# Two conditional residual layers on one core: layer 0 as four 64x64 array tiles, two pairs per block and two pairs ahead

## The reference

```python
# layer 0, per batch b: subject s = itok_B_0_7[b] of 8
x = x + einsum('bct,bcd->bdt', x, weights[s]) + bias[s][:, :, None]   # weights[s]: 64 x 64
# layer 1, per batch b: adapter a = itok_B_0_6[b] of 8
H = einsum('btd,od->bto', x, W)                                      # W: 512 x 512
xa = einsum('btd,brd->btr', x, A[a])                                 # rank 16
delta = einsum('btr,bor->bto', xa, Bm[a]) * scalings[a]
x = x + H + delta
```

## Time and profile before

| | us |
|---|---|
| three executions | 275.54, 275.44, 274.51 |
| median | 275.44 |
| span of the profiled execution, first to last instruction | 271.8 |
| PE busy in that span | 256.0 |
| DVE busy | 148.6 |
| ACT busy | 113.3 |
| POOL busy | 87.9 |

### The profile page before, as it was taken

The page is one execution under the profiler, slowest core; times in us unless marked ns, Lnnn a source line. Parts: engine busy times, 40 slices in busy tenths (PEclk is TensorE's granted clock), DMA queues, the critical chain, the costliest instruction groups (busy, mean ns, idle before and its releaser), DMA issues.

```text
span 271.8 us, 6814 instructions
## 1 busy us (share of the span) xinstructions
PE 256.0 (94%) x1393; PEld 220.1 (81%) x1394; DVE 148.6 (55%) x244; ACT 113.3 (42%) x189; POOL 87.9 (32%) x285
## 2 busy tenths in 40 slices
PE   0598999999999999999999999999999999999993
PEld 0476888888888888888888888888888888888882
DVE  5668677555655556555665566555655553344300
ACT  2254554433544354433444353443434433323511
POOL 7355223433333332333432342333332333330000
PEclk9999999999999999999999999999999999999998
DMA  6662554454554545444554455543655455455221
GB/s 122 160 164 59 158 145 144 129 148 123 168 137 134 153 135 154 136 134 133 170 141 129 141 144 154 146 128 114 171 147 143 131 152 156 138 144 148 63 55 39
DMA packets 25821, 36.62 MB, mean 135 GB/s; under 512 B 6736, under 2 KB 8784, under 8 KB 25808
## 3 DMA queue, kind: packets, MB, share of 16 engines
q1 hardware_dynamic: 20400, 28.06, 37.1%
q10 hardware_dynamic: 5408, 8.40, 11.9%
HBM read 19.67 MB, written 16.78 MB: 134 GB/s over the span
## 4 chain that ended last, share of the span: by engine, by line
PE 91%; DVE 3%; DMA 3%; ACT 1%; issue 1%; SPq 0%; ACTq 0%; DVEq 0%
PE ps L696 66%; PE ps L682 21%; PE ps L671 3%; DMA a_f<-in_L_cond_A_dram 2%; DMA ids_i<-in_itok_B_dram 1%; PE ps L653 1%; DVE x_lo L494 1%; DVE m_lo L481 1%; PE ps L643 0%; ACT x_hi L559 0%; DVE prec_n L382 0%; DVE a_parts L460 0%; DVE m_f L475 0%; ACT m_hi L553 0%; ACT a_parts L542 0%
## 5 line engine op out<-in xcount | busy, mean ns | idle before, releaser
L696 PE MATMUL ps<-m_hi,x_hi 128*128 x264 | 108.6, 411 | 0.8 <-DVE x_lo L494 0.4
L696 PE MATMUL ps<-m_lo,x_hi 128*128 x264 | 103.1, 390 | 0.0
L696 PE MATMUL ps<-m_hi,x_lo 128*128 x264 | 103.1, 390 | 0.0
L353 POOL COPY p_pair<-p_all 64x64 f32 x128 | 52.0, 406 | 149.8 <-issue 73.3
L682 PEld LDWEIGHTS ps<-p_pair,x_ring 128*128 128x128 f32 x512 | 67.5, 193 | 5.4 <-DMA x_ring<-in_x_dram 0.4
L494 DVE TENSOR_TENSOR x_lo<-x,x_hi 128x512 fp32r<-128x512 f32 x64 | 44.5, 695 | 47.1 <-ACT x_hi L559 47.1
L682 PE MATMUL ps<-p_pair,x_ring 128*128 128x128 f32 x512 | 68.1, 276 | 0.0
L568 ACT ACTIVATE o_ring<-ps 128x512 f32<-128x512 f32 x60 | 35.8, 596 | 74.2 <-PE ps L696 74.0
L487 DVE TENSOR_TENSOR x<-ps,bias_pair 128x512 f32<-128x512 f32 x64 | 44.2, 691 | 35.9 <-PE ps L682 35.2
L559 ACT ACTIVATE x_hi<-x 128x512 fp32r<-128x512 f32 x64 | 40.5, 632 | 43.3 <-DVE x L487 43.3
L696 PEld LDWEIGHTS ps<-m_hi,x_lo 128*128 128x128 f32 x264 | 49.6, 188 | 10.6
(11 more groups left out here) (82 smaller groups left out, 54.5 us busy)
## 6 DMA issues: line engine op xcount, KB each, us to landing
x_ring<-in_x_dram SPq DMA_DIRECT2D x128, 128.0 KB, 2.6
out_dram<-o_ring SPq DMA_DIRECT2D x64, 128.0 KB, 2.6
out_dram<-o_ring ACTq DMA_DIRECT2D x64, 128.0 KB, 2.3
o_ring<-in_L_cond_W_dram SPq DMA_DIRECT2D x4, 256.0 KB, 4.4
a_f<-in_L_cond_A_dram SPq DMA_DIRECT2D x8, 128.0 KB
b_nat<-in_L_cond_Bm_dram SPq DMA_DIRECT2D x1, 256.0 KB, 4.0
p_all<-in_L_cond_weights_dram SPq DMA_DIRECT2D x2, 128.0 KB, 4.2
bias_all<-in_fside_8xS_dram SPq DMA_DIRECT2D x1, 256.0 KB, 4.7
```

Of the source, the lines that this page charges most:

```text
L353: nc.gpsimd.tensor_copy(p_pair[rows, slot, rows], p_all[rows, ds(s[half], 1), :] .rearrange("p s d -> p (s d)")).then_inc(pair_ready, 1)
L696: mm = nc.tensor.matmul(ps[:, bank, :], part[:, u % 2, c, :], m[:, ds(k * (TC * T) + c * T, T)], start=(c == 0 and part is x1_hi and m is ...
```

## The change

`layer0` now makes 16 matmuls per pair where it made 4. Each contracts 64 partitions (`half`: one batch of the pair) and writes 64 partitions of PSUM (`side`: which 64 of the 128 time steps of the chunk), with 64 moving columns. So each works on one 64 x 64 quarter of the array. The zeros of the block diagonal are gone, and `p_pair` shrinks to 64 columns. The two halves write two different banks: 0 and 1 for even pairs, 6 and 7 for odd ones; `turn_b` moves from bank 6 to bank 4, which `m_product` also uses. `x1_add` reads the two banks and writes the same `x1` as before.

PE does layer 0 for pairs j + 2 and j + 3 in one block ahead of `layer1(j)`, j even, and none for odd j. The waits for both pairs' inputs stand ahead of the table read. `x1_hi` and `x1_lo` have four buffers (`HELD`), DVE and ACT make them two pairs ahead, and `x` is asked for six pairs ahead while its ring keeps four slots: `load_x(j + 6)` waits for layer 0 of pair j + 2.

```diff
-    AHEAD = 4
+    AHEAD = 6
+    HELD = 4
-        p_pair = sb("p_pair", [P, XR, P])
+        p_pair = sb("p_pair", [P, XR, C])
-        x1_hi = sb("x1_hi", [P, 2, TC, P], F32R)
-        x1_lo = sb("x1_lo", [P, 2, TC, P], F32R)
+        x1_hi = sb("x1_hi", [P, HELD, TC, P], F32R)
+        x1_lo = sb("x1_lo", [P, HELD, TC, P], F32R)
...
+        def l0_banks(u):
+
+            return 6 * (u % 2)
...
-                nc.vector.tensor_tensor(x1[:, u % 2], ps[:, u % 2, :].rearrange("p (c n) -> p c n", c=TC),
-                                        bias_pair[:, u % XR, :].unsqueeze(1).to_broadcast([P, TC, P]),
-                                        ALU.add).then_inc(x1_ready, 1)
+                bank = l0_banks(u)
+                nc.vector.tensor_tensor(x1[:, u % 2].rearrange("p c (h d) -> p c h d", h=2),
+                                        ps[:, bank:bank + 2, 0:TC * C].rearrange("p h (c d) -> p c h d", c=TC),
+                                        bias_pair[:, u % XR, :].rearrange("p (h d) -> p h d", h=2).unsqueeze(1)
+                                        .to_broadcast([P, TC, 2, C]), ALU.add).then_inc(x1_ready, 1)
...
             def step(j, u, n):
-                if not isinstance(j, int) or j + 1 < PAIRS:
-                    x1_add(j + 1, u + 1)
-                    x1_split(j + 1, u + 1)
+                if not isinstance(j, int) or j + 2 < PAIRS:
+                    x1_add(j + 2, u + 2)
+                    x1_split(j + 2, u + 2)
...
-                at_least(act, l1_done, j - 1)
-                nc.scalar.activation(x1_hi[:, u % 2], x1[:, u % 2], ACT.Copy).then_inc(x1_hi_ready, 1)
+                at_least(act, l1_done, j - HELD + 1)
+                nc.scalar.activation(x1_hi[:, u % HELD], x1[:, u % 2], ACT.Copy).then_inc(x1_hi_ready, 1)
...
-            def layer0(j, u):
+            def layer0_inputs(j, u):
 
                 slot = u % XR
                 pe.wait_ge(x_in[slot], after(j, u, 32))
                 pe.wait_ge(pair_ready, j * 4 + 4)
 
                 at_least(pe, x1_ready, j - 1)
+
+            def layer0(j, u):
+
+                slot = u % XR
+                bank = l0_banks(u)
                 for c in range(TC):
-                    mm = nc.tensor.matmul(ps[:, u % 2, c * P:c * P + P], x_ring[:, slot, c * P:c * P + P],
-                                          p_pair[:, slot, :], start=True, stop=True)
+                    for side in range(2):
+                        for half in range(2):
+                            rows = slice(C * half, C * half + C)
+                            at = c * P + side * C
+                            mm = nc.tensor.matmul(ps[side * C:side * C + C, bank + half, c * C:c * C + C],
+                                                  x_ring[rows, slot, at:at + C], p_pair[rows, slot, :],
+                                                  start=True, stop=True)
                 mm.then_inc(l0_done, 1)
...
+                if u % 2 == 0 and (not isinstance(j, int) or j + 2 < PAIRS):
+                    layer0_inputs(j + 2, u + 2)
+                    layer0_inputs(j + 3, u + 3)
                 k = words(pe, regs[:2 if mixed else 1], table[0:1, ds(j * 8 + W_PLACE, 2 if mixed else 1)], K - 1)
-                if not isinstance(j, int) or j + 1 < PAIRS:
-                    layer0(j + 1, u + 1)
+                if u % 2 == 0 and (not isinstance(j, int) or j + 2 < PAIRS):
+                    layer0(j + 2, u + 2)
+                    layer0(j + 3, u + 3)
```

More of the change, by code:

```diff
@@ L258, in _ @@
             sp.wait_ge(batches_ready, 1)
-            for j in range(AHEAD):
+            for j in range(XR):
                 load_x(j, j, words(sp, regs[:2], table[0:1, j * 8:j * 8 + 2], B - 1))
             load_a(1)
+            for j in range(XR, AHEAD):
+                load_x(j, j % XR, words(sp, regs[:2], table[0:1, j * 8:j * 8 + 2], B - 1))
             def step(j, u, n):
@@ L310, in _ @@
             nc.gpsimd.memset(b_dup[:], 0.0).then_inc(consts, 1)
+            pool.wait_ge(consts, 12)
+            nc.gpsimd.memset(a_parts[GR:P, :].bitcast(F32), 0.0).then_inc(consts, 1)
             pool.wait_ge(consts, 13)
-            nc.gpsimd.memset(a_parts[GR:P, :].bitcast(F32), 0.0).then_inc(consts, 1)
-            pool.wait_ge(consts, 14)
             pool.wait_ge(bnat_in, 16)
@@ L352, in place_p @@
                     rows = slice(C * half, C * half + C)
-                    nc.gpsimd.tensor_copy(p_pair[rows, slot, rows], p_all[rows, ds(s[half], 1), :]
+                    nc.gpsimd.tensor_copy(p_pair[rows, slot, :], p_all[rows, ds(s[half], 1), :]
                                           .rearrange("p s d -> p (s d)")).then_inc(pair_ready, 1)
@@ L388, in _ @@
             iota_done = did(nc.vector.tensor_copy(iota[:], iota_i[:]))
[L390 removed]
+            dve.wait_ge(consts, 6)
             nc.vector.tensor_copy(ones_b[:], ones[:]).then_inc(consts_b, 1)
@@ L486, in x1_add @@
                 at_least(dve, x1_lo_ready, j - 1)
[L487 to L489 removed]
+                bank = l0_banks(u)
[3 more added lines that the diff above has]
+                                        .to_broadcast([P, TC, 2, C]), ALU.add).then_inc(x1_ready, 1)
             def x1_split(j, u):
                 dve.wait_ge(x1_hi_ready, j + 1)
[L494 removed]
+                nc.vector.tensor_tensor(x1_lo[:, u % HELD], x1[:, u % 2], x1_hi[:, u % HELD],
                                         ALU.subtract).then_inc(x1_lo_ready, 1)
[L498 removed]
+            dve.wait_ge(consts, 13)
             b_split(0)
@@ L510, in _ @@
             m_split(3, 3)
+            x1_add(1, 1)
+            x1_split(1, 1)
             def step(j, u, n):
-                if not isinstance(j, int) or j + 1 < PAIRS:
-                    x1_add(j + 1, u + 1)
-                    x1_split(j + 1, u + 1)
+                if not isinstance(j, int) or j + 2 < PAIRS:
+                    x1_add(j + 2, u + 2)
+                    x1_split(j + 2, u + 2)
                 for place_at, chunk in split_at(j, u, n):
@@ L611, in _ @@
             m_round(3, 3)
+            x1_round(1, 1)
             act.wait_ge(batches_ready, 1)
             def step(j, u, n):
-                if not isinstance(j, int) or j + 1 < PAIRS:
-                    x1_round(j + 1, u + 1)
+                if not isinstance(j, int) or j + 2 < PAIRS:
+                    x1_round(j + 2, u + 2)
                 if makes_parts(j, u, n) is not None:
@@ L695, in layer1 @@
                     for part, m in ((x1_hi, m_hi), (x1_hi, m_lo), (x1_lo, m_hi)):
-                        mm = nc.tensor.matmul(ps[:, bank, :], part[:, u % 2, c, :],
+                        mm = nc.tensor.matmul(ps[:, bank, :], part[:, u % HELD, c, :],
                                               m[:, ds(k * (TC * T) + c * T, T)],
@@ L708, in _ @@
             turn_w(2)
+            layer0_inputs(0, 0)
             layer0(0, 0)
@@ L713, in _ @@
             pe.wait_ge(others_ready, 2)
+            layer0_inputs(1, 1)
+            layer0(1, 1)
             regs = [pe.alloc_register(f"pe_word{i}") for i in range(2)]
```

16 lines of the change are left out of this document (7 added, 9 removed).

## The result

The changed kernel takes 265.52 us in the median of four executions (263.79 to 268.1), the kernel before 274.98 in four of its own (273.92 to 275.54). The ratio is 0.9645, 95% interval 0.9613 to 0.9677: 9.5 us faster by these medians, where 17.0 were forecast. (The ratio leaves out the execution of 268.1 us, which fell in a slower state of the chip; without it the changed kernel's median is 265.2.) The time lies in the range, and in the likeliest case's own. The profiled span went from 271.8 to 264.2 us, by 7.6.

The account below looks back on a forecast made before the run. PE's stream was taken as the bound. Layer 0 goes from 54.3 to 30 x (0.89 + 0.33) = 36.6 us, the start adds 0.7: span 271.8 to 254.8, plus 3.6 gives 258.4 us; range 248 to 292 us.

Parts of the forecast that it names:

- likeliest case: All four quarters of PE's array working at a time in layer 0: 248 to 270 us, chance 0.38.
- What bounds the kernel: Steady part: the chain of waits runs on PE alone, so every nanosecond off PE's stream comes off the end.
- Four at a time: Layer 0 on PE: four quarters overlap, so a block's 64 passes take 0.89 us against 1.78; chance 0.38.
- rival 1: Layer 0 passes begin strictly in order, two quarters at a time: block 1.78 us, total 285 us; chance 0.33.
- The seams: Changing the array's division before and after each block empties PE's pipeline: 2 x 165 ns = 0.33 us a block.
- Steady sum: Layer 0 on PE's path: 54.3 us before, 30 x (0.89 + 0.33) = 36.6 after.
- The start: First block of two waits for POOL's pair 3 copies; pair 0's delay costs nothing, later adapter parts cost 0.7 us once.
- No queue is passed by a late step: Engine queues: the waits moved ahead of the table read are met long before, so no late step delays others; costed at nothing.
- The cover becomes thin: DVE per two pairs: 6.0 us with its waits for ACT, against a new period of 6.7; still covered.
- rival 4: DVE's chain becomes the bound, a few tenths of a us a block, some 5 us: 263 us; chance 0.04.
- From span to time: The median of the runs is 3.6 us above the profiled span, kept for the changed kernel: 254.8 becomes 258.4 us.
- Costed at nothing: x1_add's shorter runs, x1 parts two pairs ahead, POOL's copies and loads of x all stay hidden: 0 us.

Follow-up runs that it names:

- schedule_only: The kernel before with blocks of two pairs, two pairs ahead, four buffers, x six ahead, but layer 0 still in 128 x 128 matmuls: 281.67 us.
- start_late: The changed kernel with layer 1 of pair 0, then the B transpose, put ahead of the first block of two at the start: 263.08 us.
- start_pool: start_late with POOL copying the next adapter's B one pair later, behind the pair's own copies: 262.33 us.
- early_a: start_pool with SP asking for the next adapter's A two pairs earlier: 261.03 us.
- tiles_only: The kernel before with layer 0 as 16 matmuls of 64 x 64 in every step, one pair ahead, two buffers: 270.55 us.

## Why the prediction was right, and where not

- **What bounds the kernel**: right. The gain in the steady part is PE's, and PE stays busy: in the stretch from 98 to 128 us for all of 30.00 us, and from 52 us on with one wait, of 0.55.
- **Four at a time**: right. 0.95 us for 0.89. The rows I had at hand (two small matmuls 0.02 us apart) allowed 1.3. The Trainium skill (TensorE: Matmul & The Clock Gate, Part 3) has matmuls strictly first in, first out, by which I had rival 1. That a second pass on the same quarter would hold back the next quarter's start is refuted by the 15 ns. Whether passes start in program order is doubtful here: each matmul's two passes stand next to each other in it and take 58 ns each on their quarter, yet four passes start within 20 ns. The records don't name the quarter, so this isn't shown; that passes end in order no run contradicts.
- **The seams**: right, 0.34 for 0.33. The Trainium skill (TensorEngine Tiling, Key Properties) says that a change of mode empties the engine; the traces agree in so far as both seams cost time: 0.34 us for the two of a block, and 0.40 for each block more, against nothing in schedule_only, which has the same blocks and one mode. That an emptying is what costs it, as in my 2 x 165 ns, isn't shown: the three pieces (0.09, 0.135, 0.11) are none of them 0.165.
- **Steady sum**: 61 x 0.89 - 30 x 1.29 = 15.6 us less, forecast 17.7: each block costs 0.07 more.
- **The start: the step that failed.** I wrote that the first block "waits for POOL's copies for pair 3" and that "pair 0's delay costs nothing", + 0.7 us in all. I missed the third wait in `layer0_inputs(3)`: `x1_ready` of pair 1. With it the block begins at 25.69 and not at 21.3, and the span gains 7.6 us where the steady sum has 15.6: 8.0 are lost, 0.55 of them in the later wait, the rest in the start. Schedule_only shows most of the loss without the quarters (+ 7.0 us, 5.4 of them in the start); start_late and its two followers win back 4.5 of it. Part of it is the clock, 2.2 us behind the wait. Its mean over a stretch is no measure of the loss: from 16 to 28 us it is 0.69 here, 0.86 in schedule_only, 0.72 in start_late, and 1.00 in start_pool and early_a as before, while the profiled spans of start_late and start_pool are 262.4 and 262.7 us.
- **"No queue is passed by a late step"** was wrong as well: the waits now stand at PE's head, with the table read and layer 1 behind them. In start_pool SP's late A reached PE by just this way. "The cover becomes thin" was right: rival 4 was there, in small, by way of the late A.
- **From span to time**: I kept 3.6 us between them. The executions with both numbers have 1.7 (265.84 and 264.2 in the changed kernel, 274.88 and 273.2 in one of before), so the profiled execution of before was a short one, if its own difference was 1.7 too; its time isn't on record. It is why the span fell by 7.6 and the medians by 9.5.
- **The range held in part by luck.** The 7.5 us that are missing from the forecast of 17.0 are 2.1 of the steady sum and 7.3 of the start (8.0 for 0.7), less 1.9 that the 3.6 us above gave back. The range was made for overlap and seams; for the start it had nothing but the + 0.7, and its width took the miss in.
- **Costed at nothing**: four buffers and x six ahead do have to be there. Leaving out the one costs 37 us, the other 161.

Still open: the rest of the start, some 3.5 us. In part it can be read from early_a's waits of PE, 4.0 us in the four lines above, where the kernel before has 1.4 (0.6 for `a_parts`, 0.4 for `m_lo`, 0.4 for `x1_lo`). Putting the table read back ahead of the waits is the nearest experiment that wasn't made. In most kernels with quarters the first layer 0 also waits longer for x (0.9 to 1.5 us, 1.4 in the changed kernel) than in schedule_only (0.2) and before (0.4, for its weight load). No run tells why. That two pairs could be kept apart in one bank by columns, which would take the block's wait away, wasn't tried: DVE would then read a bank while PE writes it, which no kernel here does.

## What to carry to other kernels

Small fp32 products like these (64 x 64 x 64) are worth putting on the four quarters of the array, in an order that changes the quarter at least every four passes, better every two, and in blocks long enough to pay for the seams (0.34 to 0.40 us a block here). When an engine does more work per visit, list every wait that now stands at the head of its queue, in the first round above all, and what else stands between those waits and the work: the steady sum can be right to 0.07 us a block while the first block gives back half of the gain. A deeper buffer or an earlier request that "only" adds reserve is priced by what stands in order behind the wait that it removes.

## What the runs showed of the hardware that I had not expected

- fp32 passes on four quarters follow at 15 ns on average, in groups of four every 58 ns, with two passes of the same quarter next to each other in program order; four in a row still go at 17 ns or so (block 1.24 us), eight don't (2.62, 41 ns).
- Divided by rows alone, with 128-column loads and 64 moving columns, the two halves work side by side, but each pass takes 111 to 112 ns, as an undivided one with 128 moving columns does; the block is longer than the undivided one (1.93 us against 1.78).
- In a wait of PE of 1.4 us the granted clock already fell to 0.50, the lower of its two levels (0.57 in the mean from 17 to 18 us), and the wait of 4.5 us was followed by a block of 1.99 us in place of 1.09. The length of one wait doesn't tell: in tiles_only the clock was at 0.50 after a wait of 0.9 us for x (at 17.03 us), in early_a it stayed at 1.00 in the table after a wait of 1.3 us (at 14.83). What PE did between differs too: four transposes at 15.46 us took 0.60 in tiles_only, four at 15.85 took 1.05 in early_a, so there PE hadn't been fast before.
